# State space scan: GpSimd makes six mixes instead of five, VectorE the first and the last, the first-half gates go through PSUM, and one projection tile stands between the sums of squares

## The reference

```
zxbcdt = h @ in_proj_w.T                   # z gates, xs inputs, B, C, dt
...
def step(hprev, inp):                      # the state space scan over the 36 tokens of an image
    hn = hprev * dA_t + dtx_t * B_t
    return hn, einsum(hn, C_t)
y = ys + D_skip * xs                       # skip
y = y * silu(z)                            # gate
y = y * rsqrt(mean(y * y) + EPS) * ssm_norm_w
x = x + y @ out_proj_w.T                   # projection
h2 = layer_norm(x)
f = h2 @ fc1_w.T; f = f[:H] * silu(f[H:])
return x + f @ fc2_w.T
```

## Time and profile before

| | |
|---|---|
| timed runs | 358.98, 359.0, 354.08 us (median 358.98) |
| profiled execution, device time | 353.49 us |
| its span | 351.7 us |
| mean granted TensorE clock | 0.995 of full |
| TensorE busy | 328.9 us, 94% of the span |
| VectorE busy | 184.0 us, 52% |
| ScalarE busy | 137.3 us, 39% |
| GpSimd busy | 92.8 us, 26% |

### The profile page before, as it was taken

One profiled execution on the slowest core, in us unless ns is written; L12 is line 12 of the kernel. 1 busy time (PEld: TensorE's weight loads), 2 busy tenths in 40 slices (PEclk: granted clock), 3 DMA queues, 4 the chain that ended last, 5 costly groups with the idle time before them and its releaser, 6 DMA issues.

```text
span 351.7 us, 6861 instructions
## 1 busy us (share of the span) xinstructions
PE 328.9 (94%) x2593; PEld 256.0 (73%) x2607; DVE 184.0 (52%) x512; ACT 137.3 (39%) x287; POOL 92.8 (26%) x124
## 2 busy tenths in 40 slices
PE   4999999989897999899898998889999999999996
PEld 1999895636643454546667857669999999999995
DVE  2798696876553433388976625581225221621225
ACT  2999422782422122347882234321221221321320
POOL 8199824000023421013060010004233233212110
PEclk9999999999999999999999999998999999999999
DMA  6954149997979894170089992202499999999222
GB/s 213 413 101 115 7 120 290 258 243 200 270 273 356 209 279 112 42 192 2 1 207 265 239 245 57 75 3 75 113 289 284 284 262 260 250 243 255 83 76 88
DMA packets 31746, 64.57 MB, mean 184 GB/s; under 512 B 10817, under 2 KB 17506, under 8 KB 31714
## 3 DMA queue, kind: packets, MB, share of 16 engines
q1 hardware_dynamic: 29506, 59.38, 62.8%
q0 software_dynamic: 1920, 4.56, 4.7%
q10 hardware_dynamic: 288, 0.20, 0.2%
HBM read 54.74 MB, written 4.65 MB: 169 GB/s over the span
## 4 chain that ended last, share of the span: by engine, by line
PE 72%; DVE 9%; POOL 6%; ACT 5%; issue 3%; DMA 3%; SPq 0%; DVEq 0%; ACTq 0%; POOLq 0%
PE ps L1898 13%; PE ps L1923 10%; PE ps L1910 7%; PE ps L1623 6%; PE ps L1689 4%; PE ps L2022 3%; PE ps L1631 3%; PE ps L1987 3%; PE ps L1695 2%; PE ps L1997 2%; PE ps L1772 2%; DMA xg<-token_x,src_id 2%; POOL tot L111 2%; PE ps L1875 1%; POOL xsq L617 1%
## 5 line engine op out<-in xcount | busy, mean ns | idle before, releaser
L690 POOL DMA_INDIRECT xg<-token_x,src_id x22 | 21.4, 974 | 119.6 <-DVE src_id L1360 76.6
L1389 DVE TENSOR_TENSOR ht<-sg,ps 128x384 f32<-128x384 f32 (+1 forms) x48 | 23.8, 509 | 50.9 <-ACT sg L908 49.1
L1623 PE MATMUL ps<-busy 128*128 128x512 bf16 x157 | 44.8, 392 | 5.8 <-POOL ident L600 4.5
L1898 PE MATMUL ps<-xgt,wup 128*128 128x128 f32 x384 | 47.3, 281 | 0.0
L1898 PEld LDWEIGHTS ps<-xgt,wup 128*128 128x128 f32 x384 | 46.5, 198 | 0.4 <-issue 0.4
L908 ACT ACTIVATE sg<-ps 128x384 f32<-128x384 f32 (+1 forms) x48 | 21.0, 455 | 49.6 <-PE ps L1910 34.3
L1631 PEld LDWEIGHTS ps<-weff,xp 128*128 128x128 f32 x240 | 39.2, 190 | 1.3 <-DVE weff L1044 1.1
L1631 PE MATMUL ps<-weff,xp 128*128 128x193 f32 x240 | 39.9, 327 | 0.2 <-ACT xp L751 0.2
L1923 PE MATMUL ps<-wdn,ht 128*128 128x192 f32 x192 | 35.2, 334 | 0.0
L697 POOL DMA_INDIRECT token_y<-ysb,row_id x20 | 19.7, 985 | 54.9 <-ACT ysb L915 54.9
L1923 PEld LDWEIGHTS ps<-wdn,ht 128*128 128x128 f32 x192 | 30.8, 190 | 1.8
(11 more groups left out here) (353 smaller groups left out, 574.4 us busy)
## 6 DMA issues: line engine op xcount, KB each, us to landing
w<-in_m_w SPq DMA_DIRECT2D x24, 384.0 KB, 6.7
wup<-in_m_w SPq DMA_DIRECT2D x16, 576.0 KB, 7.9
wup<-in_m_w SPq DMA_DIRECT2D x48, 192.0 KB, 8.6
wdn<-in_m_w SPq DMA_DIRECT2D x16, 576.0 KB, 12.0
w<-in_m_w SPq DMA_DIRECT2D x36, 128.0 KB, 6.2
xw<-in_xw SPq DMA_DIRECT2D x2, 784.0 KB, 10.9
wall<-in_w_sh SPq DMA_DIRECT2D x2, 768.0 KB, 9.3
token_y<-busy SPq DMA_DIRECT2D x2, 480.0 KB, 4.1
```

What stands on the lines that cost most here:

```text
L690: g.indirect_dma_start(xg[:, j, :], None, token_x[m], bass.IndirectOffsetOnAxis(ap=src_id[:, j:j + 1], axis=0))\
L1389: v.tensor_tensor(ht[:, j % 2, s, 0:half], sg[:, s, 0:half], ups, ALU.mult)\
L1623: mm(ps[:, bank, :], busy[:, 0:P], busy[:], start=True, stop=True)
L1898: mm(ps[:, 2 * s + g, c * P:c * P + P], up[:, col:col + P], xgt[:, 0, j * P:j * P + P], start=(c == 0), stop=False)
```

## The change

Three edits, and nothing else. GpSimd makes the mixes of pairs 1 to 6 in this order, VectorE those of pairs 0 and 7. The first-half gates write their intermediate into the PSUM bank that they read, in place of `yt`; gate 0 stands behind the `dtx` of pair 6, and gates 1 and 2 behind `dtx` and mix of pair 7. On TensorE `projected(0)` takes the place of the six matmuls on zeros between the two parts of `squares`; it waits for the three first-half gates (`v_yz` at 3) and for the scaled weights (`g_wout`).

```diff
-WARM_SCAN, WARM_GATE = (6, 2, 3), 6
-MIX_POOL = (1, 3, 5, 6, 7)
+WARM_SCAN = (6, 2, 3)
+MIX_POOL = (1, 2, 3, 4, 5, 6)
 MIX_DVE = tuple(j for j in range(PAIRS) if j not in MIX_POOL)
...
                 v.scalar_tensor_tensor(
-                    out=yt[:, r, half].rearrange("p (i n) -> p i n", n=NTOK),
+                    out=ps[:, 2 * r, 0:HB].rearrange("p (i n) -> p i n", n=NTOK),
                     in0=xst[:, r, 0:8, 0:NTOK], scalar=dskip[:, r:r + 1],
                     in1=ps[:, 2 * r, 0:HB].rearrange("p (i n) -> p i n", n=NTOK),
                     op0=ALU.mult, op1=ALU.add).then_inc(S["v_ys"], 1)
                 dve.wait_ge(S["v_ys"], r + 1)
-                v.tensor_tensor(yt[:, r, half], yt[:, r, half], zs[:, r, half], ALU.mult).then_inc(S["v_yz"], 1)
+                v.tensor_tensor(yt[:, r, half], ps[:, 2 * r, 0:HB], zs[:, r, half], ALU.mult).then_inc(S["v_yz"], 1)
...
-                if j >= PAIRS - HP:
+                if j >= PAIRS - 2:
                     dve.wait_ge(S["p_ys"], 1)
-                    gated(j - (PAIRS - HP), 0)
+                    for r in ((0,), (1, 2))[j - (PAIRS - 2)]:
+                        gated(r, 0)
...
             squares(0, (0, 1))
-            keep_busy(6, WARM_GATE)
+            pe.wait_ge(S["g_wout"], 1)
+            pe.wait_ge(S["v_yz"], HP)
+            projected(0)
             pe.wait_ge(S["g_ssm"], 6)
             squares(1, (2, 3, 4)).then_inc(S["p_ssq"], 1)
-            pe.wait_ge(S["g_wout"], 1)
             pe.wait_ge(S["v_yz"], 2 * HP)
-            for t in range(TT):
+            for t in range(1, TT):
                 projected(t)
```

## The result

The changed kernel's median is 357.44 us over 20 executions, that of before 355.75 over 20. The forecast for the change was -0.7 us. With more runs the two groups of before filled in to one spread, 353.36 to 360.75 us.

The account below looks back on a forecast made before the run. TensorE, busy 72% of the span, was taken as the bound, with `scanned(0)`'s start deciding. It starts 0.72 us earlier and the tail follows: 353.49 - 0.72 = 352.8 us profiled, 358.98 - 0.7 = 358.3 us timed; range 352.3 to 359.9.

Parts of the forecast that it names:

- Where TensorE is the bound, and what VectorE does: Scan and gates: `dtx` 6 waits for TensorE's transposes until about 185.38 us; VectorE's second-half gates start at 189.58.
- the 0.16 us which mixes and gates lose: VectorE's gates: second half starts at 189.58 us instead of 189.42, so VectorE ends 0.16 us later.
- Gates through PSUM at 0: First-half gates: writing the intermediate to PSUM was taken to cost 0; worst case 0.25 us per gate.
- The projection tile, 0.72 us earlier: Between the sums of squares: the tile replaces the zeros, and `scanned(0)` moves from 195.08 to 194.36 us.
- rivals 2 and 3: First-half gates: PSUM writes cost 0.25 us each, no change, 10%; PSUM reads cost 0.05 us more each, -0.57, 5%.
- rival 1: Behind the scan: TensorE's clock falls without the zeros; one 1.82 us stretch less the 0.72 gain, +1.1 us; 10%.
- The whole tail moves with it: From layer norm through fc1, routing and experts to the end: everything comes 0.72 us earlier.
- The level: Whole kernel: two of three timed runs were in the upper group, so 358.98 - 0.7 = 358.3 us.
- The range's top of 359.9: Whole kernel: upper end of the range, 359.0 + 1.1 rounded down to 359.9 us; all cases within it, 95%.

Follow-up runs that it names:

- mixes_only: Kernel of before with only the mix and gate edits; six matmuls on zeros between the sums and all projection tiles behind them; ratio to before 1.001.
- sbuf_gates: Changed kernel with six matmuls on zeros in TensorE's waits, and first-half gates through SBUF (`yt`) instead of PSUM; ratio to before 0.999.
- holes_filled: Changed kernel plus six matmuls on zeros in TensorE's waits: three ahead of the last scan, three in the first sums; ratio to before 0.9977.
- tile_only, tile_only: Kernel of before with the third edit alone: first projection tile in place of the six matmuls on zeros; ratio to before 1.0031.
- holes_sums: Changed kernel plus three matmuls on zeros in the waits of the first sums, none ahead of the last scan; ratio to before 0.9952.
- mixes_sums: Mix and gate edits alone, the six matmuls on zeros kept, plus three more in the waits of the first sums; ratio to before 1.0009.
- sums_again: Changed kernel with three matmuls on zeros in the waits of the first sums, measured once more; ratio to before 0.998.
- holes_scan: Changed kernel plus three matmuls on zeros in the wait ahead of the last scan, none in the first sums; ratio to before 1.0004.
- after_zeros: Changed kernel plus six matmuls on zeros right behind the first projection tile; 352.83 and 356.58 us, before's median 354.55.

## Why the prediction was wrong

- **Where TensorE is the bound, and what VectorE does**: right to 0.03 us at the starts named above, up to the second-half gates, and the 0.16 us which mixes and gates lose shows in mixes_only.
- **Gates through PSUM at 0**: right, 0.01 each to write. L1530 takes 0.457 us reading PSUM (`ps,zs`) and 0.457 reading SBUF (sbuf_gates), so rivals 2 and 3 fell.
- **The projection tile, 0.72 us earlier**: right as a mechanism, with 0.65 in holes_filled, but only with the clock held. The missing 0.07 is in the second sums: the working starts them at 191.8 and gives them 1.90 us, so they end 0.17 earlier, where their row has 2.06; in holes_filled they start and end 0.09 earlier than before, counted from L1512. The sum took TensorE's durations at a granted 1.00 from the earlier trace rows and used them for a program from which the dense part had been taken.
- **The step that failed** is in rival 1: "`projected(0)` is dense too", and the clock "stood at 1.00 there". It stood there with the matmuls on zeros. tile_only has the clock fall with the tile in their place, and mixes_only has it hold with them back. I gave this 10%. Of the changed kernel's executions only that of 822.79 us has a mean clock above 0.990, while 53 of the 110 of before beside the experiments have 0.995 or more: it was the rule. Its price was also too low: I took one stretch of 1.82 us, and the profile has half clock for 7 us, 2.5 us late at L1165 against the forecast, +1.8 net instead of +1.1. The 1.82 itself compares two different expert tiles; the same one takes 2.87 us at full clock, so the stretch costs 1.63 there.
- **The whole tail moves with it**: the 1.8 us were still there at the end, but luck had a part in it: the expert tile around 240 us cost the same in both profiles, once by the lower clock and once by the 1.69 us, and other profiles have neither.
- **The level**: 358.3 was set by the upper group of three runs, and 20 executions have it at 355.75. The measured 357.44 is in the range, but for the wrong reason: the sign was wrong. The range's top of 359.9 also lay under rival 1's own 360.1.

What stays open: why three zeros in the sums hold the clock while three ahead of the last scan do not; and what the 1.69 us around 244 us are, which the profiles of tile_only, mixes_sums and sums_again show too.

## What to carry to other kernels

A matmul on zeros that is on the critical path isn't idle time to be handed out: before real work takes its place, read the granted clock behind that place in a profile of the changed kernel; here it was 0.50. Durations read at full clock are good for a forecast only if the clock stays: the same 24 projection records took 4.15 us at 1.00 in `holes_sums` and 6.73 in the changed kernel. Fillers in TensorE's waits among the first sums held it here (mean clock 0.996 in `holes_sums`, 0.984 in the changed kernel) and cost nothing, since the scan and the sums started no later (the last scan 11.92 us behind L1512 in both profiles, the second sums 15.67). Fillers ahead of the last scan (0.987 in `holes_scan`) or behind the tile (0.50 from 192 to 195 us in the profile of `after_zeros`) did not. With the fillers among the sums the loss of 0.6% was gone: the two measurements of that kernel against before gave 0.9952 and 0.998, the second with 1 in its interval. The gain shown by a cause is 0.65 us, 0.2%. The changed kernel itself wasn't timed beside it.

## What the runs showed of the hardware

- TensorE that the trace shows busy throughout lost its clock: from 192 to 194 us of the changed kernel its busy share was 1.00, first with 192-column and then with one-column matmuls, and the clock fell from 1.00 to 0.50 in the next microsecond. The longest wait in the 7 us ahead of the fall was 0.73 us.
- VectorE writing its result to PSUM and not SBUF: 0.515 us (changed kernel) against 0.506 (sbuf_gates) for 288 columns. Reading one operand from PSUM and not SBUF: 0.457 us both ways, in the same two.
- A mix of VectorE's, with both operands in SBUF, took 0.60 us with GpSimd idle (changed kernel), and 1.51 and 1.55 where it started while GpSimd was on one of its own (before). Where VectorE's started first, it took 0.61 and GpSimd's 1.53 in place of 1.11 (the changed kernel's first). A `dtx`, which reads PSUM, took 0.56 us among GpSimd's mixes and 0.55 behind them (changed kernel, at 181.09 and 188.42).
